# A two-layer decoder on one core: the first mixture's rows carry weight and number, each expert norms and scatters its own output, the next stage's weights are loaded early, and the second cross attention hands its maxima over without DRAM

## The reference, cut to what matters

```
x = x + mamba_A(layernorm(x))
x = x + xattn_0(layernorm(x), ctx)          # 16 heads, no softmax, then an MLP
x = x + ffn_0(layernorm(x))                 # one expert of 8 per row, at most 512 rows each
x = x + mamba_B(layernorm(x))
x = x + xattn_1(layernorm(x), ctx)          # causal softmax, 16 heads of 16
x = x + ffn_1(layernorm(x))                 # two experts of 8 per row, and a shared one

# ffn_0, N = 2048 rows, E = 8 experts, capacity 512:
x_flat = x @ W_proj + b_proj
tok_weight, tok_expert = top1(softmax(x_flat @ W_gate)); tok_weight /= tok_weight
h = gelu(layernorm(x_flat[top_idx] @ W1[e] + b1[e]) * ln1_g[e] + ln1_b[e])
out_e = (h @ W2[e] + b2[e]) * weight
outputs = zeros(N, 256).at[top_idx].add(out_e)
return layernorm(outputs) * ln_g + ln_b
```

## Time and profile before

| | |
|---|---|
| median of 3 runs | 2972.07 us (2971.61 to 2978.2) |
| profiled execution | 2965.96 us, span 2964.2 us |
| PE busy | 2423.3 us (82%) |
| DVE busy | 2196.2 us (74%) |
| ACT busy | 1443.9 us (49%) |
| POOL busy | 893.1 us (30%) |
| chain that ended last | PE 46%, DVE 28%, ACT 11%, issue 8%, DMA 3%, POOL 2% |
| mean granted TensorE clock | 0.903 of full |

### The profile page before, as it was taken

How to read it: one execution, slowest core, us unless ns; L and a number is a source line. 1 busy time by engine, 2 the same in 40 slices (tenths; PEclk the granted TensorE clock), 3 DMA queues, 4 the chain that set the end, 5 groups by cost and what they waited for, 6 DMA issues and landing times.

```text
span 2964.2 us, 31542 instructions
## 1 busy us (share of the span) xinstructions
PE 2423.3 (82%) x10888; PEld 1578.0 (53%) x10888; DVE 2196.2 (74%) x3180; ACT 1443.9 (49%) x2547; POOL 893.1 (30%) x617
## 2 busy tenths in 40 slices
PE   4979886588998899937992698888667879799998
PEld 1333332367776566737882234343233434789998
DVE  5999999698985564337886599999955643567776
ACT  5666474255664222215653665656402435347774
POOL 2868776200000000020002377777601223200004
PEclk7999999899998899968996799999987876889999
DMA  4032130570000000022421312303056241246652
GB/s 168 1 114 77 38 115 0 176 245 1 23 1 1 34 1 1 0 105 96 148 82 43 137 37 78 114 2 114 0 138 123 53 94 48 85 149 216 218 204 90
DMA packets 100067, 249.58 MB, mean 84 GB/s; under 512 B 9426, under 2 KB 63583, under 8 KB 91960
## 3 DMA queue, kind: packets, MB, share of 16 engines
q1 hardware_dynamic: 83540, 222.64, 23.3%
q0 software_dynamic: 4608, 12.59, 1.3%
q10 hardware_dynamic: 11760, 12.32, 1.3%
HBM read 194.42 MB, written 53.10 MB: 84 GB/s over the span
## 4 chain that ended last, share of the span: by engine, by line
PE 46%; DVE 28%; ACT 11%; issue 8%; DMA 3%; POOL 2%; ACTq 1%; SPq 0%; DVEq 0%; POOLq 0%
DVE psum L635 10%; PE psum L432 6%; PE psum L109 5%; PE psum L111 5%; PE psum L110 5%; PE psum L116 3%; DVE ch L643 3%; PE psum L397 3%; ACT WH L3101 2%; ACT g L3248 2%; PE psum L1265 2%; PE psum L1279 2%; PE psum L1249 2%; PE psum L1227 1%; PE psum L2535 1%
## 5 line engine op out<-in xcount | busy, mean ns | idle before, releaser
L317 POOL TENSOR_TENSOR bu<-u,row 128x1024 f32<-128x1024 f32 x254 | 597.2, 2356 | 289.0 <-DVE psum L635 189.8
L432 PE MATMUL psum<-ch,ident 128*128 128x512 f32 x1024 | 510.2, 627 | 139.9 <-DVE ch L643 139.4
L635 DVE TENSOR_TENSOR_SCAN psum<-psum,bu 128x1024 f32<-128x1024 f32 x256 | 585.5, 2287 | 18.9 <-ACT psum L514 18.7
L432 PEld LDWEIGHTS psum<-ch,ident 128*128 128x128 f32 x1024 | 187.7, 196 | 428.8 <-DVE ch L643 247.6
L514 ACT ACTIVATE psum<-dt,A 128x511 f32<-128x511 f32 x512 | 332.4, 682 | 0.4
L643 DVE TENSOR_TENSOR ch<-psum,row 128x1024 f32<-128x1024 f32 x256 | 312.8, 1222 | 7.6
L1535 POOL IOTA i<- 128x128 f32 x1 | 0.3, 345 | 710.3 <-DVEq L3393 710.3
L397 PE MATMUL psum<-hT,inw 128*128 128x512 f32 x256 | 138.2, 672 | 43.4 <-ACT sz L474 27.3
L3248 ACT ACTIVATE g<-psum,bias 128x256 f32<-128x256 f32 x248 | 101.1, 470 | 130.8 <-PE psum L111 126.8
L109 PE MATMUL psum<-WH,hs 128*128 128x256 f32 x496 | 144.9, 292 | 4.8 <-DVE hs L3328 2.3
L109 PE MATMUL psum<-xT,WH 128*128 128x256 f32 x496 | 141.0, 284 | 7.6 <-DVE xT L3291 7.6
(11 more groups left out here) (403 smaller groups left out, 5888.1 us busy)
## 6 DMA issues: line engine op xcount, KB each, us to landing
W<-in_m1W SPq DMA_DIRECT2D x24, 2052.0 KB, 8.6
row<-Ascr SPq DMA_DIRECT2D x64, 512.0 KB, 4.7
row<-Bscr SPq DMA_DIRECT2D x64, 512.0 KB, 4.8
m1buf<-zt SPq DMA_DIRECT2D x8, 2048.0 KB, 16.7
W<-in_m0W SPq DMA_DIRECT2D x16, 1024.0 KB, 5.2
WH<-x1scr SPq DMA_DIRECT2D x16, 384.0 KB, 8.1
x1scr<-hi SPq DMA_DIRECT2D x48, 128.0 KB, 2.4
qk<-x1scr SPq DMA_DIRECT2D x16, 384.0 KB, 8.4
```

The source lines that it names most:

```text
L317: e.tensor_tensor(m.bu[i % 3][:, :, :], u, m.row[:, g, 0, :, :], ALU.mult).then_inc(*m.fed.up)
L432: p = pe.matmul(m.y, k.ident, m.ch[i % RING_C][:, j, :], start=False, stop=g == UNITS - 1 and j == 1)
L635: dve.tensor_tensor_scan(flat, flat, m.bu[i % 3][:, :, :].rearrange("p a n -> p (a n)"), 0.0, ALU.mult, ALU.add).then_inc(*m.scan.up)
```

## The change

In the first mixture a row in `m0buf` has 258 columns: the row, its weight and its number. Each expert's output is normed at once (statistics of the unweighted output; weight, mean and inverse are combined by small POOL operations), multiplied by ln_g, and scattered by POOL to its row of `m0res`, which is cleared beforehand. The stage ends when all scatters have landed; mamba B's SP program loads `m0res` in four parts into its tile `row`, and VectorE adds them to X and takes the statistics there. ln_b is added to X by POOL. Half of each weight's low part is made by POOL. The statistics of the hidden rows are taken tile by tile. In the last expert the products with W2 go block by block between the turns. Mamba B's weights are loaded during expert 2. In the second cross attention maxima and ones are copied from SBUF to SBUF, the maxima's copy stands ahead of the next queries' spill, the scatters stand in other slots, and the last batch's units are spread over 15 slots instead of 22.

```diff
     sp.dma_start(m.dtw[:, :], d[L + "dtw"]).then_inc(*m.w.up)
     sp.dma_start(m.outw[:, :, :], d[L + "outw"]).then_inc(*m.w.up)
+def mamba_home(m, b):
+    return m.row[:, b, 0, :, :].rearrange("p a (t c) -> p (a t) c", c=D)
+def mamba_sp(k, m, sp):
+    if m.rnd:
+        for b in range(B):
+            sp.dma_start(mamba_home(m, b), k.DR["m0res"][T * b:T * b + T, :].rearrange("(t p) c -> p t c", p=128)).then_inc(*m.home_in[b].up)
+        sp.wait_ge(*m.home(B - 1))
+    else:
+        mamba_weights_sp(k, m, sp)
     for b in range(B):
         sp.wait_ge(*m.drawn(mamba_use("xp", b, 0)))
         sp.dma_start(m.scr[b], m.xd[m.R:m.R + 32, :]).then_inc(*m.spilled.up)
@@ -521,6 +537,8 @@
         act.wait_ge(*k.mean_var(0))
         act.activation(m.t0[:, 0:4], k.xmv[:, 0:4, 1], ACT.Sqrt).then_inc(*m.dev.up)
     act.activation(m.A[:, :], pv(k, L + "A_log", 64), ACT.Exp).then_inc(*m.a_exp.up)
+    if m.rnd:
+        x_stats_act(k, act, 4 * m.rnd)
     mamba_item_act(k, m, act, "h", 0, 0)
     mamba_item_act(k, m, act, "h", 0, 1)
     for j in range(12):
@@ -530,9 +548,9 @@
     g.then_inc(*m.diag.up)
     for j in range(4):
         mamba_item_act(k, m, act, "in", 0, j)
-    if m.rnd == 0:
-        for j in range(1, B):
...
+    for j in range(1, B):
+        x_stats_act(k, act, 4 * m.rnd + j)
+    if m.rms:
         act.activation(m.t0[:, 4:NT], k.xmv[:, 4:NT, 1], ACT.Sqrt).then_inc(*m.dev.up)
     mamba_silu_act(k, m, act, 0)
...
 
+def mamba_home_dve(k, m, dve, b):
+    x = k.X[:, 4 * b:4 * b + 4, :]
+    dve.wait_ge(*m.home_in[b](0))
+    dve.tensor_tensor(x, x, mamba_home(m, b), ALU.add).then_inc(*m.home.up)
+    dve.wait_ge(*m.home(b))
+    x_stats_dve(k, dve, 4 * m.rnd + b)
 def mamba_dve(k, m, dve):
-    for b in range(B if m.rnd else 1):
-        dve.wait_ge(*k.inv_dev(4 * m.rnd + b))
+    if m.rnd:
+        mamba_home_dve(k, m, dve, 0)
+        x_inverse_dve(k, dve, 4 * m.rnd)
...
+    for j in range(1, B):
+        if m.rnd:
+            mamba_home_dve(k, m, dve, j)
+        else:
             dve.wait_ge(*k.x_in[j](0))
...
-            x_inverse_dve(k, dve, j)
-            dve.wait_ge(*k.inv_dev(j))
+    for j in range(1, B):
+        x_inverse_dve(k, dve, 4 * m.rnd + j)
+        dve.wait_ge(*k.inv_dev(4 * m.rnd + j))
+    if m.rms:
...
+    wider = k.zt[:, :, :].rearrange("p a c -> p (a c)")[:, 0:D + 2].unsqueeze(1).to_broadcast([128, 16, D + 2])
+    for j in range(TRASH // 2048):
+        sp.dma_start(k.DR["m0buf"][2048 * j:2048 * j + 2048, :].rearrange("(t p) c -> p t c", p=128), wider) \
             .then_inc(*k.cleared["m0"].up)
     for j in range(E + 1):
...
+    sp.dma_start(k.DR["m0res"][0:N, :].rearrange("(t p) c -> p t c", p=128), k.zt[:, 0:1, :].to_broadcast([128, NT, D])) \
+        .then_inc(*k.cleared["m0"].up)
     context(2)
...
         if e:
-            sp.wait_ge(*m.W1l(2 * e - 1))
+            for j in range(2):
+                sp.wait_ge(*m.W1l[j](e - 1))
         sp.dma_start(m.W1[:, :, :], d["m0W1"][e]).then_inc(*m.W1_in.up)
...
+        if e == 2:
+            mamba_weights_sp(k, following, sp)
+    for home in m.home:
+        sp.wait_ge(*home(2 * E - 1))
 
...
     pool.wait_ge(*m.put(0))
-    pool.wait_ge(*k.cleared["m0"](16))
...
+    def first_split(e):
+        pool.wait_ge(*m.W1h(2 * e + 1))
+        pool.tensor_tensor(m.W1s[1][:, 1, :], m.W1[:, 1, :], m.W1s[0][:, 1, :], ALU.subtract).then_inc(*m.W1l[1].up)
+    def second_split(e):
+        pool.wait_ge(*m.W2h(2 * e + 1))
+        pool.tensor_tensor(m.W2s[1][:, 4:8, :], m.W2[:, 4:8, :], m.W2s[0][:, 4:8, :], ALU.subtract).then_inc(*m.W2l[1].up)
+    def tags(e):
+        pool.wait_ge(*m.xe_in(e))
+        if e == 0:
+            pool.wait_ge(*m.rooms(0))
+        pool.tensor_tensor(m.tf[:, e, :], m.room[:, e, :], m.xe[:, :, D + 1], ALU.add).then_inc(*m.tf_in.up)
+        pool.tensor_copy(m.tw[:, e, :], m.xe[:, :, D])
+        pool.tensor_tensor(m.t2[:, e, :], m.xe[:, :, D], m.xe[:, :, D], ALU.mult)
+        pool.tensor_scalar(m.tn[:, e, :], m.xe[:, :, D], -1.0, None, ALU.mult)
+        pool.wait_ge(*m.tf_in(e))
+        pool.tensor_copy(m.ti[:, e, :], m.tf[:, e, :]).then_inc(*m.tagged.up)
+    def out_var(e):
+        pool.wait_ge(*m.tagged(e))
+        pool.wait_ge(*m.o_mv(e))
+        if e:
+            pool.wait_ge(*m.o_sc(e - 1))
+        pool.tensor_tensor(m.osd[:, :], m.omv[e % 2][:, :, 1], m.t2[:, e, :], ALU.mult).then_inc(*m.o_var.up)
+    def out_scale(e):
+        pool.wait_ge(*m.o_rec(e))
+        pool.tensor_tensor(m.nsc[:, :], m.osd[:, :], m.tn[:, e, :], ALU.mult).then_inc(*m.o_neg.up)
+        if e:
+            pool.wait_ge(*m.o_n(e - 1))
+        pool.tensor_tensor(m.osc[:, :], m.osd[:, :], m.tw[:, e, :], ALU.mult)
+        pool.wait_ge(*m.o_neg(e))
+        pool.tensor_tensor(m.onb[:, :], m.nsc[:, :], m.omv[e % 2][:, :, 0], ALU.mult).then_inc(*m.o_sc.up)
+    def out_home(e, t):
+        pool.indirect_dma_start(k.DR["m0res"], bass.IndirectOffsetOnAxis(ap=m.ti[:, e, t:t + 1], axis=0), m.ob[e % 2][:, t, :], None) \
+            .then_inc(*m.home[e % 2].up)
+    first_split(0)
+    second_split(0)
+    tags(0)
+    tags(1)
+    first_split(1)
+    pool.wait_ge(*m.vecs(1))
+    for e in range(E):
+        if e < B:
+            x = k.X[:, 4 * e:4 * e + 4, :]
+            pool.tensor_tensor(x, x, m.vec["ln_b"][:, :].unsqueeze(1).to_broadcast([128, 4, D]), ALU.add).then_inc(*m.xb.up)
+        if e + 2 < E:
+            tags(e + 2)
+        if e:
+            out_scale(e - 1)
+        if e + 2 < E:
+            first_split(e + 2)
+        if e:
+            ob = m.ob[(e - 1) % 2][:, :, :]
+            pool.wait_ge(*m.o_n(e - 1))
+            pool.tensor_tensor(ob, ob, m.vec["ln_g"][:, :].unsqueeze(1).to_broadcast([128, 4, D]), ALU.mult).then_inc(*m.o_g.up)
+            pool.wait_ge(*m.o_g(e - 1))
+            for t in range(4):
+                out_home(e - 1, t)
+        if e + 1 < E:
+            out_var(e)
+            second_split(e + 1)
+    for t in range(4):
+        pool.wait_ge(*m.o_last(t))
+        out_home(E - 1, t)
 
 
 def hidden_pe(k, m, pe, e):
-    pe.wait_ge(*m.W1l(2 * e + 1))
+    for j in range(2):
+        pe.wait_ge(*m.W1l[j](e))
     pe.wait_ge(*m.xl(2 * e + 1))
...
+def last_out_pe(k, m, pe, e, o):
+    if o == 0:
+        for j in range(2):
+            pe.wait_ge(*m.W2l[j](e))
+    pe.wait_ge(*m.hl(8 * e + o))
+    for t in range(4):
+        p = mm3(pe, k.psum[:, 4 + t, 0:D], [h[:, o, 128 * t:128 * t + 128] for h in m.hs], [w[:, o, :] for w in m.W2s], o == 0, o == 7)
+        if o == 7:
+            p.then_inc(*m.o_at.up)
 
 
...
+            if e + 1 == E and o:
+                last_out_pe(k, m, pe, e, o - 1)
         step(rows)
+        if e + 1 == E:
+            last_out_pe(k, m, pe, e, 7)
+            break
...
+        for j in range(2):
+            pe.wait_ge(*m.W2l[j](e))
         for t in range(4):
...
+    def out_dev(e):
+        act.wait_ge(*m.o_var(e))
+        act.activation(m.osd[:, :], m.osd[:, :], ACT.Sqrt, bias=k.eps).then_inc(*m.o_sd.up)
+    def out_rows(e):
+        act.wait_ge(*m.o_sc(e))
+        for t in range(4):
+            o = m.ob[e % 2][:, t, :]
+            a = act.activation(o, o, ACT.Identity, scale=m.osc[:, t:t + 1], bias=m.onb[:, t:t + 1])
+        a.then_inc(*m.o_n.up)
 
...
+        if e:
+            out_dev(e - 1)
         if e + 1 < E:
             hidden_norm(e + 1)
         if e + 2 < E:
             first_split(e + 2)
-        for t in range(4):
-            own.use()
+        if e:
+            out_rows(e - 1)
         if e + 1 < E:
+            for t in range(4):
...
             second_split(e + 1)
-        act.wait_ge(*m.o_in(4 * e + 3))
-        act.dma_start(k.DR["m0res"][CAP * e:CAP * e + CAP, :].rearrange("(t p) c -> p t c", p=128), m.ob[e % 2][:, :, :]) \
-            .then_inc(*m.stored[e % 2].up)
-    def weighted(b):
...
+    out_dev(E - 1)
...
-            dve.tensor_tensor(m.W1s[1][:, j, :], m.W1[:, j, :], m.W1s[0][:, j, :], ALU.subtract).then_inc(*m.W1l.up)
+        dve.wait_ge(*m.W1h(2 * e))
+        dve.tensor_tensor(m.W1s[1][:, 0, :], m.W1[:, 0, :], m.W1s[0][:, 0, :], ALU.subtract).then_inc(*m.W1l[0].up)
 
...
             dve.wait_ge(*m.o_at(4 * (e - 1) + 3))
-        for j, o in enumerate((0, 4)):
-            dve.wait_ge(*m.W2h(2 * e + j))
-            dve.tensor_tensor(m.W2s[1][:, o:o + 4, :], m.W2[:, o:o + 4, :], m.W2s[0][:, o:o + 4, :], ALU.subtract).then_inc(*m.W2l.up)
+        dve.wait_ge(*m.W2h(2 * e))
+        dve.tensor_tensor(m.W2s[1][:, 0:4, :], m.W2[:, 0:4, :], m.W2s[0][:, 0:4, :], ALU.subtract).then_inc(*m.W2l[0].up)
...
+            dve.wait_ge(*m.hb(n))
             for j in range(2):
                 s = dve.bn_stats(st[:, t, 6 * j:6 * j + 6], hN[:, t, 512 * j:512 * j + 512])
-        s.then_inc(*m.h_st.up)
-        yield
+            if t == 3:
+                s.then_inc(*m.h_st.up)
+            yield
 
     def hidden_norm(e):
...
+    def out_stats(e):
+        seen = []
+        for t in range(4):
```

(60 more changed lines are left out.)

147 lines of the change are left out of this document (49 added, 98 removed).

## The result

The changed kernel takes 2954.09 us (median of 6 runs, 2950.55 to 2957.45), the kernel before 2971.84 (6 runs): ratio 0.9942, 95% interval 0.9924 to 0.996. Forecast was 2930, with 2903 to 2954 around it: faster, as forecast, but by 17.8 us instead of 42. The two profiled executions differ less than the medians, 2964.2 against 2954.3 us of span.

A forecast was written before the change was run, and what follows sets the result against it. TensorE and VectorE nearly fill the expert loop; the seam behind it is nearly empty. Terms 0.4 - 6.0 + 0 - 24.5 - 12.3 = -42.4 give 2923.6 us profiled, 2930 for the runs; range 2903 to 2954.

The forecast's parts named there:

- Head: Routing, head and expert 0: +0.4 for routing, -4.0 ahead of expert 0's products, -2.0 inside it.
- Hidden: Routing: GpSimd's two low halves behind the scatters cost nothing before TensorE needs W1; up to 2.4 us if uncovered.
- Inside expert 0: First expert: a statistics block of 4.84 us no longer stands between two products' splits, half already hidden; -2.0 us.
- The loop: Middle experts: VectorE's lighter load offset by GpSimd blocking, no gain or loss over six transitions; ends -16 and +20 us.
- I take 5.0 us of blocking: a period of 30.0: Expert loop: GpSimd operations block VectorE's 25.0 us by 5.0, between none and 7.1, giving 30.0 us per expert.
- into the 15 us: Expert loop: some GpSimd operations fall into 15 us of VectorE operations that don't need the shared port.
- the port in full: Rival, chance 0.22: nearly every large GpSimd operation blocks VectorE; 31.0 us per expert, 33.3 with X; 2941 in all.
- The last expert: Expert 7: out products go block by block between the turns, so the last split comes 4.5 us later.
- the pace of 1.9 us a block: Last expert: half a tile's 2.87 us of out products plus four turns, against 1.33 before; eight blocks at 0.56 more.
- The seam: Last split to second stage's first convolution: GpSimd's scatter queue, then four loads; 69.4 to 44.9 us, -24.5, bounds -15 to -32.
- Attention: Second cross attention: direct SBUF copies, earlier maxima, moved scatters and packed slots; -12.3 us, bounds -3 and -21.
- The last stage: Last mixture, the final stretch of the kernel: no change forecast, 0 us.

The follow-up runs named there:

- e2: Changed kernel with W1's second low half taken back from GpSimd to VectorE; ratio 0.9885 to the kernel before.
- e3: Changed kernel with GpSimd's low halves of expert 0 ahead of its sixteen scatters instead of behind them; ratio 0.9954 to the kernel before.
- e1: Changed kernel with GpSimd's ln_g multiplication delayed until VectorE has added b2 to the next expert's first output tile; ratio 0.9919 to the kernel before.
- e8: Changed kernel with the last expert's W2 products tile by tile after its eight blocks, as before; ratio 0.9927 to the kernel before.
- f2: Changed kernel with W1's half and X on VectorE, expert 6's output early, last expert by tiles, norm steps between them, batch 1's closing units first; 0.9825 to kernel before.
- g2: Kernel before with only the change's part in the second cross attention; ratio 0.9968 to the kernel before.
- g1: Changed kernel with W1's half and X on VectorE, last expert by tiles, norm steps between them, batch 1's closing units first; ratio 0.9801 to kernel before.
- e7: Changed kernel with W1's second half and X plus ln_b on VectorE, expert 6's output normed and scattered during expert 7; ratio 0.9859 to the kernel before.

## Why the prediction was off

*Head, -5.6 forecast, +0.6 measured (and the first scatter was 1.6 sooner): wrong.* "Hidden" was said of the two halves behind the scatters by looking only at TensorE's need of them. SyncE waits for the same half before it loads expert 1's W1, and its in-order queue then put that load directly ahead of the rows': the rows' load began at 1311.84 instead of e2's 1310.09 and took 7.05 instead of 3.58, 5.2 us in all; e3 shows the length of the load alone, e2 both. From the landed rows to N0 came 2.9 us less than before (27.3 to 24.5) where 4.0 were forecast. Inside expert 0, where 2.0 were forecast, the first distance fell by 1.0, from 29.0 to 28.0, since the normed rows were already held up there; without GpSimd's half of W1 it is 25.9 (e2).

*The loop, 0 forecast, +9.7 over five transitions: wrong, and it is the larger error.* The step that failed is "I take 5.0 us of blocking: a period of 30.0". The blocking was 4.9: 2.1 at the normed rows, 2.2 at W1, 0.6 at the splits beside W2. But the period isn't VectorE's busy time. VectorE has 2.0 us of waits left per expert (31.47 less 29.43), which the sum put at nothing, and two distances have 1.8 us more with X, which I had listed and then let fall "into the 15 us". So 31.5 and 33.3 stand against 30.0. That the amount of blocking came out at 4.9 is partly luck: it was a choice between 0 and 7.1. The rival named "the port in full" gave 31.0 and 33.3; measured are 31.5 and 33.3. It was the right one for the loop, at 0.22; its total of 2941 fell short by the head and the last expert. The Trainium skill, "SBUF — State Buffer", section "Who interferes with whom", which the prediction had cited, says also that whichever of the two issues first gets the shared ports for the whole instruction. e2 agrees (GpSimd 3.82 us, VectorE undisturbed). e1 and e2 show that this order, not the amount of work, was the thing to lay out.

*The last expert, +4.5 forecast, +8.7 measured: mis-sized.* The step that failed is the pace of 1.9 us a block, which was TensorE's work at full clock and nothing else. From the first split to the last it took 18.0 us, 9.2 before, and the forecast's pace gives 13.3. Of the missing 4.7, 3.6 fall in the first three of the seven steps, two of which ran wholly or in part with TensorE's clock at half, and 1.1 in the last four, where the pace was 2.2, set by the loop of waits that e8 opens.

*The seam, 40.4 forecast from the last split on, 42.4 measured: right,* by its steps: GpSimd's queue of scatters and then the first load home, 24.5 us to X's first addition (22.4 forecast), and from there 17.9 us to the convolution (18.0 forecast).

*Attention, -12.3 forecast, -5.4 in the first two profiles, -9.5 by the ratio of the attention alone: mechanism right* (the maxima's wait gone, loads next), size within what the runs can tell. What I priced too low is that the loads were nearly as late as the row had been: 10.36 us of TensorE's wait against 10.67 before, where the sum took 4.4 off.

*The last stage, 0 forecast, +3.8 in these profiles:* not the change's, as f2 and g2 show.

In all, the attention alone gives 0.9968, the change without it 0.9989 and 0.9977: of the 30 us forecast for routing, mixture and seam came 3 to 7 (8 in the profiles). With W1's half, X, the last expert's order and the attention's units mended (g1), the whole gives 59 us instead of 18.

## What to carry over

Before work is given to GpSimd, lay both engines' operations out in time and ask who is first: beside VectorE's reads of PSUM and its statistics it was free (e1); in front of VectorE's operations with two SBUF operands it cost up to its own length, above all when GpSimd had a second operation directly behind the first. A period is an engine's busy time plus the waits it keeps; take those from the profile too. Whoever moves an operation must follow each queue that waits for it; here it was SyncE's. And a price of TensorE's work holds at one clock: in the last expert, behind a pause of 5.3 us, the first blocks were worked at half.

## What was not expected of the hardware

GpSimd's scatter took 4.50 instead of 0.96 us beside four additions of 128x1024 with both inputs in SBUF (e7): these hold up the issue of an indirect transfer, not only GpSimd's arithmetic. The 1.95 us of the earlier trace rows were the same in small. And with VectorE's two halves of W1 back to back, GpSimd waited through both (3.82 us, e2) rather than get in between, while in the changed kernel it did get in between two normed rows of some 0.8 us.
